# First batch's keys and queries placed pair by pair from SBUF to SBUF, first feed-forward loads a turn later, scores over 96 and 99 rows

## The chip, the cores and the metric

The kernel runs on one core of one Trainium2 chip. The metric is the device time of one execution in microseconds (us), as the median of the runs.

## The reference

For 16 batches of 256 tokens of width 256, the reference computes a cross-attention and a feed-forward net of eight experts:

```python
q = (layernorm(x) @ Wq + bq), k = concat([ctx1 @ Wk + bk, ctx2]), v = concat([ctx1 @ Wv + bv, ctx2])   # 16 heads of 16
x = x + softmax(q k^T / 4) v @ Wp + bp
y = layernorm(x)
cw = softmax(y @ w_router) * softmax(10 * y @ w_gating);  cw = cw / (sum(cw) + 1e-9)
out = x + sum over e of cw[e] * ((silu(y @ w_gate[e]) * (y @ w_up[e])) @ w_down[e])     # inner width 1024
```

Here x has 16 x 256 x 256 elements, ctx1 and ctx2 (fside_BxSxS_0 and ctx_1024) likewise, so a query sees 512 keys.

## The kernel before

Every matmul of 32-bit data is split into a high and a low part (names with _hi and _lo), and three products stand for one. The work is laid out in turns and steps. A turn b belongs to a batch of attention and has 32 steps; turns -2 and -1 prepare. Each engine runs its own program over the same turns and steps, in order, and they meet in semaphores, so an engine that waits holds back everything behind it in its program. A class Count holds a semaphore with the number of increments per batch, and turn.wait(engine, count, d, n) waits for the n-th of batch b + d.

In a step the attention does one score matmul eight items ahead (AHEAD = 8, line L803, queries by keys, into ps_s), whose row maximum VectorE takes (negmax, L1187), and one key matmul (L813, keys by queries, into ps_t), whose exponential ScalarE takes (L947). An item is a head and a half of the queries for the first, and a pair of heads and a quarter of the keys for the second; four items are a pair, and there are eight pairs (PAIRS). The maximum is not subtracted by an engine: POOL and TensorE turn it into three rows (mq, "qm"), which ScalarE writes below the queries in QTs, and KTs holds rows of ones in the same places, so that the key matmul subtracts it. Low parts of the exponentials (Pt_lo) and the products with the values follow.

KTs and QTs hold the operands in this form: in partitions 0 to 31, 32 to 63 and 64 to 95 the high, low and high part of the keys, and the high, high and low part of the queries, and from TOP = 96 on the three rows of the maximum with zeros below them. The score matmul contracts over 96 partitions, the key matmul over 128. The keys of a batch stand after their projection in kT_hi and kT_lo (two chunks of 128 partitions by 512 keys, each chunk with four pairs), the queries in qT_hi and qT_lo. SP stores both to memory (d_k, d_q: store_keys L439, store_queries L445) and loads them from there into KTs and QTs for four pairs at a time (place_keys L452 with 3 loads, place_queries L466 with 6). In turn -1 the two stores and the first placement are issued at steps 10 and 11, in the other turns at steps 14 to 19, and the second four pairs at steps 1 and 3 of the turn after.

Between these, a list written out by hand, ITEMS, says in which step a turn does its other parts, among them cT (step 1, ctx1 transposed for the next batch), k (step 4), v (9), xT (11), m (12, ctx2 transposed) and q (13). In turn -1 they come at the steps in FIRST_AT, cT, xT, k, m, q, v. They use two banks of PSUM in alternation (bank(one): ps_m or half of ps_o), and each waits until the item before it in the same bank has been read. ScalarE and VectorE take k out (L925, L1143) before their attention work of the same step, after they have waited for k_out, the store of the batch before.

In turn -2 SP issues the first loads: the four attention weights, biases, router weights, then three feed-forward weights (load_weights, the first unit, L531), then the constant rows of KTs from key_rows (32 rows, L432). POOL clears key_rows, QTs and others with memsets (L1199 to L1209) and VectorE writes the ones. The feed-forward net starts in turn 2 at step 19 and from there every step has one unit of it beside the attention; its first weights are taken out of stage_w by ScalarE at steps 4, 12 and 20 of turn 1. Before the scores of turn -1 TensorE runs 36 transposes that nobody reads (keep_busy).

Of the kernel before, what the change touches and what calls it, by code (L numbers as in the profile page):

```python
# [24 lines left out]
F32 = mybir.dt.float32  # L25
# [4 lines left out]
P = 128  # L30
# [6 lines left out]
def bass_xattn_moe_ffn_kernel(nc, x, ctx1, ctx2, Wq, bq, Wk, bk, Wv, bv, Wp, bp, w_router, w_gating,  # L37
# [15 lines left out]
    TOP = 3 * ROWS  # L53
    GP = PAIRS // 2
# [38 lines left out]
    with ExitStack() as ctx:  # L93
# [114 lines left out]
        rows_in = sem("rows_in"); rows_clear = sem("rows_clear")  # L208
# [15 lines left out]
        v_ps = Count("v_ps", 1); v_done = Count("v_done", 1)  # L224
        k_in = [Count(f"k_in{g}", 16 * 3) for g in range(2)]
# [21 lines left out]
        CONSTS = 7  # L247
        LAST = (START + FSTEPS) // STEPS

# [58 lines left out]
        for b in range(-2, LAST + 1):  # L308
            for step, name, k, d in items_of(b):
                joint = b * STEPS + step >= START  # L310
                one = joint or len(items) % 2 == 0
                items[b, step] = (name, k, d, one, last_in.get(one, []))
                last_in[one] = released(b, name, k, d)
                if not joint:
                    last_early = dict(last_in)
# [5 lines left out]
        def bank(one):  # L321

            return ps_m[:] if one else ps_o[:, 1, :]
# [83 lines left out]
        def _(eng):  # L407
            def first_loads():

                def load_bias(m):  # L410
                    if m < 2:
                        for c in range(DC):
                            eng.dma_start(bT[:, m, c:c + 1], (bq, bk)[m][bass.ds(c * P, P)].rearrange("(p o) -> p o", o=1)).then_inc(b_in[m], 16)
                    else:
                        eng.dma_start(bias[:, m - 2], (bv, bp)[m - 2].rearrange("(o n) -> o n", o=1)
                                      .broadcast_to([P, D])).then_inc(b_in[m], 16)

                for n, w in enumerate((Wk, Wv, Wq, Wp)):
                    if n == 2:
                        load_bias(1)  # L420
                        load_bias(2)
                    if n == 3:
                        eng.dma_start(VF[:, QT:KC, :], one(c2_v, Turn(-1), 1)).then_inc(c2_in.sem, 16)
                        load_bias(0)
                        load_bias(3)
                    eng.dma_start(wraw[:, n], w.rearrange("(c p) n -> p c n", p=P)).then_inc(w_in[n], 16)
                eng.dma_start(rraw[:, :, 0:E], w_router.rearrange("(c p) n -> p c n", p=P)).then_inc(w_in[4], 16)
                eng.dma_start(rraw[:, :, E:2 * E], w_gating.rearrange("(c p) n -> p c n", p=P)).then_inc(w_in[4], 16)
                for n in range(3):
                    load_weights(n, 0)  # L430
                eng.wait_ge(const_ready, CONSTS)
                eng.dma_start(KTs[TOP:P].bitcast(F32), key_rows[TOP:P].unsqueeze(1).broadcast_to([ROWS, PAIRS, NK])).then_inc(rows_in, 16)  # L432

# [12 lines left out]

            def place_keys(turn, d, g):

                turn.wait(eng, k_out, d, 32)
                turn.wait(eng, t_ps, d - 1, 2 * OCT * (g + 1))  # L450
                for slot, part in enumerate((0, 1, 0)):
                    eng.dma_start(KTs[slot * ROWS:(slot + 1) * ROWS, g * GP:(g + 1) * GP, :].bitcast(F32),  # L452
                                  d_k[turn.b + d, part, bass.ds(g * P, P)].rearrange("(a r) n -> r a n", r=ROWS)).then_inc(k_in[g].sem, 16)

            def place_queries(turn, d, g):

                turn.wait(eng, q_out, d, 32)
                turn.wait(eng, t_ps, d - 1, 2 * OCT * (g + 1))
                if turn.b == -1:
                    eng.wait_ge(const_ready, CONSTS)  # L460
# [10 lines left out]
            def body(turn):  # L471
                for step in range(STEPS):
# [28 lines left out]
                    first = turn.b == -1  # L501
                    if turn.has(1) and step == (10 if first else 14):
                        store_keys(turn, 1)
                    if turn.has(1) and step == (10 if first else 15):
                        store_queries(turn, 1)
                    if turn.has(1) and step == (11 if first else 17):
                        place_keys(turn, 1, 0)
                    if turn.has(1) and step == (11 if first else 19):
                        place_queries(turn, 1, 0)
                    if turn.has(0) and step == 1:  # L510
                        place_keys(turn, 0, 1)
                    if turn.has(0) and step == 3:
                        place_queries(turn, 0, 1)
# [62 lines left out]
        def _(pe):  # L576
# [177 lines left out]
            def body(turn):  # L754
                for step in range(STEPS):
# [37 lines left out]
                    if turn.has(d):  # L793
                        h, qt = i // QT, i % QT
                        if i % (4 * GP) == 0:
                            g = i // (4 * GP)
                            if turn.b + d == 0:
                                pe.wait_ge(rows_in, 16)
                            turn.wait(pe, k_in[g], d, k_in[g].per)
                            turn.wait(pe, q_in[g], d, q_in[g].per)  # L800
# [5 lines left out]
                    if turn.has(0):  # L806
                        i = step
                        pair, kc = i // KC, i % KC
                        if kc == 0:
                            turn.wait(pe, qm_done, 0, 2 * pair + 2)  # L810
                        j = turn.b * STEPS + i
                        wait_keys_read(pe, j)
                        pe.matmul(key_bank(j)[:], KTs[:, pair, kc * P:(kc + 1) * P],  # L813
                                  QTs[:, pair].rearrange("p h n -> p (h n)"),
                                  start=True, stop=True).then_inc(t_ps.sem, 1)
# [5 lines left out]
        def _(act):  # L821
# [45 lines left out]
            def body(turn):  # L867
                for step in range(STEPS):
# [49 lines left out]
                    if name in ("k", "q"):  # L918
# [4 lines left out]
                        turn.wait(act, used, 0, 32)  # L923
# [3 lines left out]
                    if name == "m":  # L927
                        turn.wait(act, m_ps, 1, 1)
                        turn.wait(act, k_out, 0, 32)
                        act.activation(kT_hi[:, :, N:NK], ps[:].rearrange("p (c n) -> p c n", n=N), ACT.Copy).then_inc(m_h.sem, 1)  # L930
                    if name == "qm":
                        turn.wait(act, qm_ps, d, k + 1)
                        for h in range(2):
                            act.activation(QTs[TOP:TOP + 3, k, h, :], ps[HS * h + ROWS:HS * h + ROWS + 3, 0:N],
# [18 lines left out]
        def _(dve):  # L953
# [113 lines left out]
            def body(turn):  # L1067
                for step in range(STEPS):
# [8 lines left out]
                    if turn.b == -2 and step == 0:  # L1077
                        dve.wait_ge(rows_clear, 1)
                        dve.memset(key_rows[TOP:TOP + 3, :], 1.0).then_inc(const_ready, 1)
# [55 lines left out]
                    if name in ("k", "q"):  # L1135
# [4 lines left out]
                        turn.wait(dve, used, 0, 32)  # L1140
# [5 lines left out]
                    if name == "m":  # L1146
                        turn.wait(dve, m_h, 1, 1)
                        turn.wait(dve, k_out, 0, 32)
# [49 lines left out]
        def _(pool):  # L1198
# [6 lines left out]
            pool.memset(key_rows[:], 0.0).then_inc(rows_clear, 1)  # L1205
# [127 lines left out]
```

## Time and profile before

| | |
|---|---|
| time, median of 3 runs | 2712.37 us (2711.29 to 2715.34) |
| the profiled execution, time and span | 2711.55 us, 2709.8 us |
| mean granted clock of TensorE | 0.991 |
| TensorE busy | 2660.4 us (98%) |
| VectorE busy | 2007.7 us (74%) |
| POOL busy | 1651.8 us (61%) |
| ScalarE busy | 1526.0 us (56%) |
| DMA engines' mean busy share by the main queue | 39.0% |
| chain that ended last | TensorE 94%, VectorE 4%, issue 1%, DMA 1% |

In a profile PE is TensorE's matmuls, PEld its weight loads, DVE VectorE, ACT ScalarE, SPq the queue of SP that issues transfers. L803 is a line of the kernel. The busy time is summed over the span; the chain is followed back from the last instruction through what released each step. A clock of 1.00 is 2.4 GHz and 0.50 is 1.2 GHz.

### The profile page before, as it was taken

The page shows a single profiled execution, that of the slowest core. Times are in us where ns is not written, and L with a number is a line of the kernel's source. Part 1 is how long each engine was busy: PE and PEld are TensorE (multiplying, and loading weights), DVE is VectorE, ACT ScalarE, POOL GpSimd, SP SyncE. Part 2 cuts the span into 40 slices and gives each one's busy share as a digit, 9 for nine tenths or more (in the row PEclk, how much of TensorE's full clock was granted, in tenths as well). Part 3 has the DMA queues.
Part 4 walks back from the last instruction along what each step waited for, and adds up shares of the span by engine and source line. Part 5 has one row for each costly group of instructions (what it writes and reads, how often), then busy time and mean ns, then how long its engine had stood idle before and what let it go on. Part 6 is the DMA issues. An engine that isn't in the chain of part 4 may idle for free.

```text
span 2709.8 us, 46807 instructions
## 1 busy us (share of the span) xinstructions
PE 2660.4 (98%) x15969; PEld 2184.3 (81%) x15969; DVE 2007.7 (74%) x3303; ACT 1526.0 (56%) x2887; POOL 1651.8 (61%) x1837
## 2 busy tenths in 40 slices
PE   6899999999999999999999999999999999999998
PEld 5578888888888888888888888888888888888887
DVE  6987777777778777777777777777787777655554
ACT  4655555555555555555555555555555555544443
POOL 4766666666656666566666566666566666655554
PEclk8899999999999999999999999999999999999999
DMA  6344434444333443433434433444333442333332
GB/s 166 101 112 122 127 100 118 132 120 123 115 118 115 120 126 115 127 109 112 131 115 131 120 116 108 125 122 131 113 105 114 126 122 88 97 107 113 108 102 82
DMA packets 298427, 315.44 MB, mean 116 GB/s; under 512 B 22096, under 2 KB 269264, under 8 KB 298192
## 3 DMA queue, kind: packets, MB, share of 16 engines
q1 hardware_dynamic: 298192, 312.45, 39.0%
q8 instruction: 130, 2.13, 0.3%
q14 instruction: 105, 0.86, 0.1%
HBM read 278.15 MB, written 33.69 MB: 115 GB/s over the span
## 4 chain that ended last, share of the span: by engine, by line
PE 94%; DVE 4%; issue 1%; DMA 1%; POOL 0%; ACT 0%; SPq 0%; POOLq 0%; DVEq 0%; ACTq 0%
PE ps_s L706 26%; PE ps_t L706 26%; PE ps_o L740 25%; PE ps_s L803 4%; PE ps_t L813 4%; PE ps_a L782 2%; PE ps_a L784 2%; PE ps_m L586 1%; PE ps_m L615 1%; DVE negmax L1187 1%; PE ps_m L604 1%; DVE Pt_lo L1059 1%; PE ps_m L659 0%; DMA d_k<-kT_lo 0%; PE ps_m L677 0%
## 5 line engine op out<-in xcount | busy, mean ns | idle before, releaser
L969 DVE SCALAR_TENSOR_TENSOR hf<-hf,ps_s 128x512 f32<-128x512 f32 x512 | 350.2, 684 | 326.7 <-ACT hf L827 324.8
L833 ACT ACTIVATE h_hi<-ps_t 128x512 fp32r<-128x512 f32 x512 | 306.1, 598 | 440.2 <-DVE ps_t L976 440.2
L1221 POOL TENSOR_TENSOR wg_lo<-stage_w,wg_hi 128x512 fp32r<-128x512 f32 x256 | 330.9, 1292 | 339.5 <-ACT wg_hi L840 337.9
L827 ACT ACTIVATE hf<-ps_s 128x512 f32<-128x512 f32 x512 | 306.4, 598 | 410.5 <-PE ps_s L706 410.5
L981 DVE TENSOR_TENSOR h_lo<-ps_t,h_hi 128x512 fp32r<-128x512 f32 x512 | 353.0, 689 | 211.9 <-ACT h_hi L833 205.6
L740 PE MATMUL ps_o<-h_lo,wd_hi 128*128 128x512 f32 x1024 | 400.1, 391 | 0.0
L740 PE MATMUL ps_o<-h_hi,wd_hi 128*128 128x512 f32 x1024 | 398.5, 389 | 0.9 <-DVE h_lo L981 0.9
L740 PE MATMUL ps_o<-h_hi,wd_lo 128*128 128x512 f32 x1024 | 398.4, 389 | 0.0
L976 DVE TENSOR_TENSOR ps_t<-hf,ps_t 128x512 f32<-128x512 f32 x512 | 356.4, 696 | 52.9 <-PE ps_t L706 6.2
L1221 POOL TENSOR_TENSOR wd_lo<-stage_w,wd_hi 128x512 fp32r<-128x512 f32 x256 | 330.8, 1292 | 93.0 <-ACT wd_hi L840 93.0
L947 ACT ACTIVATE Pt<-ps_t 128x512 f32<-128x512 f32 x512 | 305.8, 598 | 142.1 <-PE ps_t L813 134.1
L1187 DVE TENSOR_REDUCE negmax<-ps_s 128x1 f32<-128x512 f32 x512 | 347.5, 681 | 23.4 <-PE ps_s L803 22.6
L1286 POOL TENSOR_TENSOR Pt_lo<-Pt 128x512 f16<-128x512 f32 x256 | 278.8, 1089 | 130.2 <-ACT Pt L947 126.8
L1221 POOL TENSOR_TENSOR wu_lo<-stage_w,wu_hi 128x512 fp32r<-128x512 f32 x256 | 333.6, 1303 | 0.0
L706 PE MATMUL ps_s<-xh,wg_hi 128*128 128x512 f32 x1024 | 320.5, 394 | 0.9 <-DVE negmax L1187 0.9
L706 PE MATMUL ps_s<-xh,wg_lo 128*128 128x512 f32 x1024 | 319.1, 392 | 0.0
L706 PE MATMUL ps_t<-xh,wu_hi 128*128 128x512 f32 x1024 | 317.5, 391 | 1.2 <-DVE h_lo L981 1.2
L706 PE MATMUL ps_s<-xl,wg_hi 128*128 128x512 f32 x1024 | 317.7, 391 | 0.0
L706 PE MATMUL ps_t<-xh,wu_lo 128*128 128x512 f32 x1024 | 316.2, 390 | 0.0
L706 PE MATMUL ps_t<-xl,wu_hi 128*128 128x512 f32 x1024 | 315.3, 389 | 0.0
L803 PE MATMUL ps_s<-KTs,QTs 96*128 96x512 f32 x512 | 231.7, 453 | 26.6 <-DVE negmax L1187 14.2
L1059 DVE TENSOR_TENSOR Pt_lo<-Pt 128x512 f16<-128x512 f32 x256 | 251.7, 983 | 1.6 <-ACT Pt L947 1.6
(208 smaller groups left out, 4734.3 us busy)
## 6 DMA issues: line engine op xcount, KB each, us to landing
stage_w<-in_L_ffn_w_gate_dram SPq DMA_DIRECT2D x256, 256.0 KB, 2.8
stage_w<-in_L_ffn_w_up_dram SPq DMA_DIRECT2D x256, 256.0 KB, 3.1
stage_w<-in_L_ffn_w_down_dram SPq DMA_DIRECT2D x256, 256.0 KB, 2.8
KTs<-d_k SPq DMA_DIRECT2D x96, 256.0 KB, 4.9
cwb<-d_cw SPq DMA_DIRECT2D x64, 256.0 KB, 3.6
QTs<-d_q SPq DMA_DIRECT2D x192, 64.0 KB, 2.7
X<-in_x_dram SPq DMA_DIRECT2D x32, 256.0 KB, 4.5
d_k<-kT_hi SPq DMA_DIRECT2D x16, 512.0 KB, 4.1
```

The source lines that it names most:

```text
L706: mm = pe.matmul(ps[:], wt[:, c, q * P:(q + 1) * P], tok[:, c].rearrange("p k n -> p (k n)"), start=(n == 0), stop=(n == 3 * DC - 1))
L740: mm = pe.matmul(ps_o[:, c, :], wt[:, q, c * P:(c + 1) * P], hid[:], start=(at == 0 and n == 0), stop=(at == EXPERT - 1 and n == 2))
L803: pe.matmul(score_bank(j)[:], QTs[0:TOP, h // 2, h % 2, qt * P:(qt + 1) * P], KTs[0:TOP, h // 2, :], start=True, stop=True).then_inc(s_ps. ...
L827: act.activation(hf[:], ps_g[:], ACT.Tanh, scale=0.5).then_inc(tanh_done, 1)
L833: act.activation(h_hi[f % FC][:], ps_u[:], ACT.Copy).then_inc(hh_done, 1)
L947: act.activation(Pt[i % RING][:], key_bank(turn.b * STEPS + i)[:], ACT.Exp).then_inc(exp_done.sem, 1)
L969: dve.scalar_tensor_tensor(out=hf[:], in0=hf[:], scalar=1.0, in1=ps_g[:], op0=ALU.add, op1=ALU.mult).then_inc(gate_done, 1)
L976: dve.tensor_tensor(ps_u[:], hf[:], ps_u[:], ALU.mult).then_inc(hf_done, 1)
L981: dve.tensor_tensor(h_lo[f % FC][:], ps_u[:], h_hi[f % FC][:].bitcast(F32), ALU.subtract).then_inc(hl_done, 1)
L1187: dve.tensor_reduce(negmax[:, (i // 4) % 2, i % 4:i % 4 + 1], score_bank((turn.b + d) * STEPS + i)[:], AX.X, ALU.max, negate=True).then_in ...
L1221: pool.tensor_tensor(lo[:], raw_weights(n), hi[:].bitcast(F32), ALU.subtract).then_inc(wl_done, 1)
L1286: pool.tensor_tensor(Pt_lo[slot][:], Pt[slot][:], Pt[slot][:].bitcast(BF16)[:, 1::2], ALU.subtract).then_inc(lo_pool.sem, 1)
```

## The change

For batch 0, the way of keys and queries through memory is replaced. A new function, place_first, issues at step 10 of turn -1 for each of the eight pairs three copies of keys and six of queries from kT and qT to KTs and QTs, SBUF to SBUF, 72 in all; a copy of keys has 32 partitions by 512 elements and one of queries 16 by 256. TensorE waits for each pair on a semaphore of its own (first_in). In turn 0 ScalarE and VectorE wait for all eight before they overwrite the source for batch 1 (wait_stored). For the other batches the stores and loads are as before; their counts begin one batch later, hence d - 1. The item q of turn -1 gets the bank ps_t[1] and waits for no other. The three first feed-forward loads move from turn -2 to steps 20, 21 and 22 of turn 0. The constant rows are 3 instead of 32, loaded without a wait for POOL's memsets and waited for at the first key matmul, POOL doesn't clear key_rows, and the key matmul contracts over 99 partitions (USED) instead of 128; the score matmul has 96 as before.

```diff
+    USED = TOP + 3
...
+        def wait_stored(eng, turn, count):
+
+            if turn.b == 0:
+                for arrived in first_in:
+                    eng.wait_ge(arrived, 16 * 9)
+            else:
+                turn.wait(eng, count, -1, 32)
...
+                if (b, name) == (-1, "q"):
+                    items[b, step] = (name, k, d, None, [])
+                    continue
...
-            return ps_m[:] if one else ps_o[:, 1, :]
+            return ps_t[1][:] if one is None else ps_m[:] if one else ps_o[:, 1, :]
...
-                for n in range(3):
-                    load_weights(n, 0)
-                eng.wait_ge(const_ready, CONSTS)
-                eng.dma_start(KTs[TOP:P].bitcast(F32), key_rows[TOP:P].unsqueeze(1).broadcast_to([ROWS, PAIRS, NK])).then_inc(rows_in, 16)
+                eng.wait_ge(rows_set, 1)
+                eng.dma_start(KTs[TOP:USED].bitcast(F32), key_rows[TOP:USED].unsqueeze(1).broadcast_to([3, PAIRS, NK])).then_inc(rows_in, 16)
...
+            def place_first():
+
+                eng.wait_ge(k_l.sem, 2)
+                eng.wait_ge(m_l.sem, 1)
+                for pair in range(PAIRS):
+                    m, at = pair // GP, pair % GP * ROWS
+                    for slot, part in enumerate((kT_hi, kT_lo, kT_hi)):
+                        eng.dma_start(KTs[slot * ROWS:(slot + 1) * ROWS, pair, :].bitcast(F32),
+                                      part[at:at + ROWS, m, :].bitcast(F32)).then_inc(first_in[pair], 16)
+                    if pair == 0:
+                        eng.wait_ge(q_l.sem, 2)
+                        eng.wait_ge(const_ready, CONSTS)
+                    for slot, part in enumerate((qT_hi, qT_hi, qT_lo)):
+                        for h in range(2):
+                            to, row = slot * ROWS + h * HD, at + h * HD
+                            eng.dma_start(QTs[to:to + HD, pair, h, :].bitcast(F32),
+                                          part[row:row + HD, m, :].bitcast(F32)).then_inc(first_in[pair], 16)
...
-                turn.wait(eng, k_out, d, 32)
+                turn.wait(eng, k_out, d - 1, 32)
...
+                    if turn.b == -1 and step == 10:
+                        place_first()
+                    if turn.b == 0 and step >= 20 and step - 20 < 3:
+                        load_weights(step - 20, 0)
+                    if turn.b >= 0 and turn.has(1):
+                        if step == 14:
+                            store_keys(turn, 1)
...
-                        if i % (4 * GP) == 0:
+                        if turn.b + d == 0:
+                            if i % 4 == 0:
+                                pe.wait_ge(first_in[i // 4], 16 * 9)
+                        elif i % (4 * GP) == 0:
...
+                        if turn.b == 0 and i == 0:
+                            pe.wait_ge(rows_in, 16)
...
-                        pe.matmul(key_bank(j)[:], KTs[:, pair, kc * P:(kc + 1) * P],
-                                  QTs[:, pair].rearrange("p h n -> p (h n)"),
+                        pe.matmul(key_bank(j)[:], KTs[0:USED, pair, kc * P:(kc + 1) * P],
+                                  QTs[0:USED, pair].rearrange("p h n -> p (h n)"),
...
-                        turn.wait(act, used, 0, 32)
+                        wait_stored(act, turn, used)
...
-                        dve.wait_ge(rows_clear, 1)
-                        dve.memset(key_rows[TOP:TOP + 3, :], 1.0).then_inc(const_ready, 1)
+                        dve.memset(key_rows[TOP:USED, :], 1.0).then_inc(rows_set, 1)
...
-                        turn.wait(dve, used, 0, 32)
+                        wait_stored(dve, turn, used)
...
-            pool.memset(key_rows[:], 0.0).then_inc(rows_clear, 1)
```

## Rows read from the trace of the kernel before

**Rows 1.** The page, its first line.

```profile
span 2709.8 us, 46807 instructions
```

**Rows 2.** Windows: stretch, length, busy of PE PEld DVE ACT POOL, clock, DMA, GB/s.

```profile
0.00:200.00 200.00, 158.76 (x1339) 116.63 (x1340) 161.42 (x317) 112.18 (x235) 121.80 (x202) 0.90 0.48 127
200.00:2500.00 2300.00, 2299.63 (x13747) 1901.91 (x13746) 1734.73 (x2825) 1319.69 (x2487) 1423.22 (x1552) 1.00 0.39 117
```

**Rows 3.** Chain of waits, 12 to 60 us: start, length, what.

```profile
13.16 0.61 DVE kT_lo L1149
...
14.26 9.93 DMA d_k<-kT_lo
...
27.88 3.64 DMA QTs<-d_q
...
31.65 0.78 PE ps_s L803
...
39.88 0.43 PE ps_t L813
...
45.70 0.84 ACT kT_hi L925 x2
...
47.52 1.20 DVE negmax L1187 x2
...
52.42 0.23 PE ps_t L813
```

**Rows 4.** Timeline up to 17 us: start, length, instruction, [idle before, releaser].

```profile
1.54 0.53 POOL L1205 MEMSET key_rows<- 128x512 f32 x1
...
4.61 1.72 DVE L1018 TENSOR_SCALAR mv<-mv 128x2 f32<-128x2 f32 x1
...
5.54 0.77 POOL L1209 MEMSET mq<- 128x256 bf16 x2
...
13.21 0.50 PE L615 MATMUL ps_m<-xT_hi,wq_hi 128*128 128x256 f32 x2 [1.56 <-DVE kT_lo L1143]
...
15.93 0.88 DVE L1143 SCALAR_TENSOR_TENSOR qT_lo<-ps_m,bT,qT_hi 128x256 fp32r<-128x256 f32 x2 [2.18 <-ACT qT_hi L925]
```

**Rows 5.** Timeline of SP's queue: start, time to issue, transfer, count.

```profile
2.76 0.94 SPq L413 DMA_DIRECT2D bT<-in_L_xattn_bk_dram  x2
...
9.19 0.47 SPq L531 DMA_DIRECT2D stage_w<-in_L_ffn_w_down_dram  x1
...
13.85 0.37 SPq L439 DMA_DIRECT2D d_k<-kT_hi  x1
...
25.58 2.72 SPq L466 DMA_DIRECT2D QTs<-d_q  x6
...
38.29 2.81 SPq L466 DMA_DIRECT2D QTs<-d_q  x6
...
64.65 3.72 SPq L466 DMA_DIRECT2D QTs<-d_q  x6
...
122.72 0.32 SPq L495 DMA_DIRECT2D d_cw<-cwT  x1
```

**Rows 6.** The tile QTs up to 140 us, last line.

```profile
DMA to landing us min/median/max: 2.2/3.7/5.0
```

**Rows 7.** Windows of 2 us, 40 to 50 us, as rows 2.

```profile
40.00:42.00 2.00, 2.00 (x9) 1.38 (x8) 0.78 (x3) 1.45 (x3) 1.75 (x5) 0.50 0.61 181
42.00:44.00 2.00, 2.00 (x7) 1.23 (x5) 2.00 (x4) 1.88 (x5) 0.68 (x2) 0.52 0.50 144
44.00:46.00 2.00, 2.00 (x16) 1.86 (x16) 1.73 (x3) 1.18 (x4) 1.85 (x2) 1.00 0.00 0
...
48.00:50.00 2.00, 1.33 (x4) 0.60 (x4) 2.00 (x5) 1.64 (x5) 1.14 (x3) 1.00 0.00 0
```

**Rows 8.** Weight loads of lines L803 and L813: ns min/median/max.

```profile
L803 PEld LDWEIGHTS ps_s<-KTs,QTs x512: 186/188/338, 31.6 to 2319.7; 96*128 96x128 f32 x171
...
L813 PEld LDWEIGHTS ps_t<-QTs,KTs x512: 186/191/338, 39.2 to 2356.4; 128*128 128x128 f32 x171
```

More of the change, by code:

```diff
@@ L207, in bass_xattn_moe_ffn_kernel @@
         w_in = [sem(f"w_in{n}") for n in range(5)]; b_in = [sem(f"b_in{m}") for m in range(4)]; b_scaled = sem("b_scaled")
-        rows_in = sem("rows_in"); rows_clear = sem("rows_clear")
+        rows_in = sem("rows_in"); rows_set = sem("rows_set")
         ident_done = sem("ident_done"); const_ready = sem("const_ready")
@@ L224, in bass_xattn_moe_ffn_kernel @@
         v_ps = Count("v_ps", 1); v_done = Count("v_done", 1)
+        first_in = [sem(f"first_in{p}") for p in range(PAIRS)]
         k_in = [Count(f"k_in{g}", 16 * 3) for g in range(2)]
@@ L245, in bass_xattn_moe_ffn_kernel @@
         cwT_ps = Count("cwT_ps", 1); cwT_done = Count("cwT_done", 1)
-        CONSTS = 7
+        CONSTS = 6
         LAST = (START + FSTEPS) // STEPS
+        def wait_stored(eng, turn, count):
[4 more added lines that the diff above has]
+                turn.wait(eng, count, -1, 32)
         class Turn:
@@ L455, in place_queries @@
             def place_queries(turn, d, g):
-                turn.wait(eng, q_out, d, 32)
+                turn.wait(eng, q_out, d - 1, 32)
                 turn.wait(eng, t_ps, d - 1, 2 * OCT * (g + 1))
-                if turn.b == -1:
-                    eng.wait_ge(const_ready, CONSTS)
                 pairs = slice(g * GP, (g + 1) * GP)
@@ L500, in body @@
                         combine_ahead(f)
[L501 to L513, printed above, removed]
+                    if turn.b == -1 and step == 10:
[5 more added lines that the diff above has]
+                            store_keys(turn, 1)
+                        if step == 15:
+                            store_queries(turn, 1)
+                        if step == 17:
+                            place_keys(turn, 1, 0)
+                        if step == 19:
+                            place_queries(turn, 1, 0)
+                    if turn.b >= 1 and turn.has(0):
+                        if step == 1:
+                            place_keys(turn, 0, 1)
+                        if step == 3:
+                            place_queries(turn, 0, 1)
                     if step in (10, 12) and turn.closed is not None:
@@ L794, in body @@
                         h, qt = i // QT, i % QT
-                        if i % (4 * GP) == 0:
+                        if turn.b + d == 0:
+                            if i % 4 == 0:
+                                pe.wait_ge(first_in[i // 4], 16 * 9)
+                        elif i % (4 * GP) == 0:
                             g = i // (4 * GP)
[L797 to L800, printed above, removed]
+                            turn.wait(pe, k_in[g], d - 1, k_in[g].per)
+                            turn.wait(pe, q_in[g], d - 1, q_in[g].per)
                         j = (turn.b + d) * STEPS + i
@@ L928, in body @@
                         turn.wait(act, m_ps, 1, 1)
-                        turn.wait(act, k_out, 0, 32)
+                        wait_stored(act, turn, k_out)
                         act.activation(kT_hi[:, :, N:NK], ps[:].rearrange("p (c n) -> p c n", n=N), ACT.Copy).then_inc(m_h.sem, 1)
@@ L933, in body @@
                         for h in range(2):
-                            act.activation(QTs[TOP:TOP + 3, k, h, :], ps[HS * h + ROWS:HS * h + ROWS + 3, 0:N],
+                            act.activation(QTs[TOP:USED, k, h, :], ps[HS * h + ROWS:HS * h + ROWS + 3, 0:N],
                                            ACT.Copy).then_inc(qm_done.sem, 1)
@@ L1147, in body @@
                         turn.wait(dve, m_h, 1, 1)
-                        turn.wait(dve, k_out, 0, 32)
+                        wait_stored(dve, turn, k_out)
                         dve.tensor_tensor(kT_lo[:, :, N:NK], ps[:].rearrange("p (c n) -> p c n", n=N),
```

## The prediction

> **What bounds the kernel now.** I read the page first: the span is 2709.8 us [rows 1], and the profiled execution took 2711.55 us, 1.75 us of it around the span. That is 0.82 us under the median of the three runs, 2712.37 us, so I add 0.8 us at the end. Next the windows: from 200 us to 2500 us TensorE is busy for 2299.63 of 2300 us, so nothing there waits, and an edit that moves only loads can gain nothing there. In the first 200 us TensorE is busy 158.76 us [rows 2]. So what this change gives or takes is a shift of the first turns, carried unchanged to the end.
>
> Then the chain of waits over the start [rows 3]. The low half of the first keys is ready at 13.77 us (0.61 us from 13.16). The chain then goes through the store of the keys (9.93 us), through the issues of the placement, through a load of queries (3.64 us), and the first score starts at 31.65 us. Turn 0 begins about 39.88 us; ScalarE takes the keys of batch 1 out of their bank at 45.70 us. That last row is my yardstick: whatever shifts it shifts the end, for VectorE's low half of the same keys and its next maximum stand behind it, and TensorE's next scores behind those; VectorE's maximum comes 0.98 us after the 0.84 us of kT_hi, at 47.52 us.
>
> **The change, part by part.**
>
> *Earlier keys.* A small VectorE operation on mv, two elements wide, takes 1.72 us from 4.61; it ends at 6.33 us, when POOL's last memset ends (5.54 + 0.77 = 6.31). So I read it as held up by POOL, and taking out the memset of key_rows (0.53 us) shortens that row of memsets by about 0.5 us [rows 4]. Everything up to the keys follows those operations, so I put SP's start on them at 13.85 - 0.5 = 13.35 us [rows 5]. At worst that gain is 0.
>
> *Earlier queries.* The first query matmul waited 1.56 us for kT_lo, because both used one bank [rows 4]. With a bank of its own it starts 1.56 + 0.5 us earlier, and qT_lo ends at 16.81 - 2.06 = 14.75 us [rows 4].
>
> *The placement.* Six large store and load steps through memory become 8 pairs x 9 = 72 DMAs on SP, in one row, with SP doing nothing else meanwhile. What does one cost to issue? Six loads of queries take 2.72 us at 25.58 and 2.81 us at 38.29; with one more gap of 0.04 us (from 13.85 + 0.37 to 14.26 [rows 3, 5]) that is 0.460 and 0.475 each, in the mean 0.467 us. Two bias columns of 0.5 KB take 0.94 us, also 0.47 each, so size hardly matters. Lowest row: 0.32 us for d_cw, whose tile spans 8 partitions, with the gap 0.36. Highest row: 3.72 us for six behind a backlog, 0.62. I take 0.467, for these have 16 or 32 partitions like the query loads (16) and are seldom behind a backlog. The three keys of pair 0 end at 13.35 + 1.4 = 14.75, just when the queries are ready, so SP doesn't wait. The last of the 72 starts at 13.35 + 71 x 0.467 = 46.51 us.
>
> Its landing: query loads of 64 KB land in 2.2 us at least, 3.7 in the median, 5.0 at most, in the first 140 us [rows 6]. SBUF to SBUF doesn't occur. The last one has 16 KB and little beside it (288 KB per 4.2 us is 69 GB/s), so I take 2.3, with 2.2 and 5.0 as ends. All is placed at 48.81 us.
>
> The Trainium skill (DMA: Bandwidth & Descriptors, section Anatomy of one DMA, given for the other DMA path) puts a fixed cost of about 2.0 us on a DMA besides its bytes; as an estimate that would make the shift below 0.3 us smaller, and no row here shows it for this path.
>
> *Who waits.* The first scores profit. Pair 0 is issued by 17.6 us and lands at 13.35 + 8 x 0.467 + 2.3 = 19.4 us, and pair 1 4.2 us later, at 23.6; four more scores with the normalisation between take about 4.9 us, so turn 0 begins near 28.5 us, 11.4 us earlier than at 39.88. Each further pair comes every 4.2 us, and turn 0 takes one only every four steps (5.8 us from 39.88 to 45.70), so the scores don't wait. But the keys of batch 1 at step 4 of turn 0 overwrite kT_hi and kT_lo, which are now the source of the placement, and wait_stored makes ScalarE and VectorE wait there for all 72. They arrive at 28.5 + 5.8 = 34.3 us and wait until 48.8. Behind that wait stand ScalarE's exponential of step 4 and VectorE's maximum of score 12, and TensorE stops two scores later, since it needs both. So the gain of 11.4 us is given back whole, and more: kT_hi starts at 48.86 us in place of 45.70, 3.2 us later. The break-even is an issue of 0.467 - 3.16 / 71 = 0.42 us.
>
> *The clock of TensorE.* In the kernel before it is granted 0.50 (1.2 GHz) in the stretch 40 to 42 us and 0.52 in the next, and 1.00 (2.4 GHz) from 44 us on [rows 7]. TensorE had stood idle until 31.65 us, worked with gaps until about 40, and without a gap from there to the rise. At the low level a key matmul takes 0.43 us of the chain, at the high one 0.23 [rows 3]. The slow steps before 45.70 no longer cost anything, as they lie ahead of the wait. Instead TensorE stands still for over 10 us and starts at low clock right after it, where before it ran at 1.00. If the clock again rises after about 3.9 us of gapless work (40.1 to 44), that is 1.95 us of full-speed work lost, less the 0.67 us in which TensorE was idle in the stretch 48 to 50 us [rows 7]: 1.3 us. Bounds: 0 if VectorE hides it, 3.5 us if the rise takes twice as long.
>
> *What is behind the 72 on SP.* The loads of x and ctx1 for batch 2 now start at about 47 us; x is wanted at step 23 of turn 0, 19 steps of 1.45 us (5.8 / 4) after the wait at step 4, and ctx1 in turn 1. The load of ctx2 waits for POOL's split at step 7 anyway. Cost 0. If that cover were gone, one landing of about 3 us.
>
> *The feed-forward loads* leave the start (three issues, the last at 9.19 us [rows 5], 768 KB) and come at steps 20 to 22 of turn 0, three issues of 0.47 us, ahead of the load of X1, which is then 1.4 us later, and wanted four steps on. ScalarE wants the first weights at step 4 of turn 1, sixteen steps after. Cost 0; the start they leave is priced by the short landings above. The constant rows shrink from 512 KB to 48 KB and are issued ahead of the inputs: 0.
>
> *Contraction over 99 rows instead of 128.* Weight loads of 96 and of 128 rows take 188 and 191 ns in the median [rows 8]. The stage from 200 us on would move only if the matmul did, and it streams the same 512 columns. I take 0; with 512 of them even the 3 ns would be 1.5 us, the lower bound.
>
> **Sum.** 3.2 + 1.3 = 4.5 us on 2711.55 gives 2716.0, and with the 0.8 us to the median 2716.8 us, 0.17% slower. What a measurement of this kernel can tell from no change is about 0.2%, 5.4 us, so the likeliest outcome is not to be told apart, on the slow side.
>
> **Rivals.**
>
> *Issues are cheap: faster.* If a DMA of 16 or 32 partitions is issued in 0.36 us, like d_cw, everything is placed at 13.35 + 25.6 + 2.3 = 41.2 us, kT_hi starts 4.5 us earlier than before, and with the 1.3 us for the clock and 1.5 us from the weight loads the time is 2712.4 - 4.5 + 1.3 - 1.5 = 2707.7 us. It is faster than before below 0.42 us (below 0.40 if the clock costs 1.3). For it: the row of d_cw. Against: all rows with 16 or more partitions, even the 0.5 KB ones. The Trainium skill says that the sequencer's time to start a DMA is usually small beside the DMA itself (DMA: Bandwidth & Descriptors, section Issuing engines are not separate DMA queues); the trace does not agree for such sizes, 0.47 us each against a landing of 2.2. Chance of a gain over 0.2%: 0.08.
>
> *The wait doesn't bite.* If step 4 came after the last landing anyway, the 11.4 us would stay, 2701.0 us. It would need turn 0 to begin 14 us later than I find. This is part of the 0.08.
>
> *The queue backs up or the clock stays low.* With 0.51 us per issue, as the issue of 0.47 us at 9.19 gives with its gap [rows 5], the shift is 3.2 + 3.1 = 6.3 us; with up to 3.5 us for the clock it is 9.8 us: 2722.2 us. At 0.62 us it would be 14 us and more, 2727. For it: six loads that took 3.72 us [rows 5]. Against: that was behind 1.5 MB of stores, just issued. Chance of over 5.4 us in all: 0.36.
>
> *The same within 0.2%:* 0.56, which holds the forecast and small gains at issues of 0.40 to 0.42. Taken together I expect 2710 to 2722.
>
> **What would show it.** In the profile after: 72 DMAs on SP from about 13.4 to 47 us with 0.467 us spacing; the first score at about 19.5 us; a wait of ScalarE and VectorE of about 14 us ahead of the kT_hi of batch 1, which starts at 48.9 us; TensorE's clock at half when it resumes; the same durations for the matmuls on KTs and QTs; TensorE still without a gap from 200 us on. I am wrong if the spacing of issues is below 0.42 or above 0.52, if small copies queue and land later than 3 us, or if the low clock lasts longer than 4 us after the wait.

## The result and the profile after

The changed kernel takes 2732.05 us (median of 6 runs) against 2711.14 us for the kernel before (6 runs): 20.9 us slower, ratio 1.0075 with a 95% interval of 1.0062 to 1.0088. The prediction had 2716.8 us, 2710 to 2722 us, and most of its chance on no difference that can be told. The sign and the mechanism are right, the size is four to five times the forecast, and the time lies outside the range.

The page after, its first lines and its clock row, answers to [rows 1]:

```profile
span 2732.3 us, 46878 instructions
## 1 busy us (share of the span) xinstructions
PE 2669.1 (98%) x15969; PEld 2194.4 (80%) x15969; DVE 2006.9 (73%) x3303; ACT 1526.7 (56%) x2887; POOL 1653.3 (61%) x1836
...
PEclk7889999999999999999999999999999999999999
```

The busy times are those of before within 9 us of TensorE; the span is 22.5 us longer. So the work is the same and something waits. The stage from 250 us on shows where it isn't (columns as in [rows 2]):

```profile
40.00:50.00 10.00, 1.99 (x39) 1.45 (x38) 0.00 (x0) 0.00 (x0) 0.73 (x4) 0.81 0.17 43
50.00:60.00 10.00, 0.00 (x0) 0.00 (x0) 0.00 (x0) 0.00 (x0) 0.00 (x0) 0.50 0.22 54
60.00:64.00 4.00, 0.00 (x0) 0.00 (x0) 0.94 (x3) 2.32 (x6) 0.94 (x1) 0.50 0.47 141
64.00:70.00 6.00, 5.42 (x18) 4.53 (x19) 4.34 (x7) 2.59 (x6) 4.05 (x9) 0.50 0.04 11
70.00:74.00 4.00, 3.98 (x52) 2.96 (x50) 3.51 (x7) 2.91 (x7) 1.40 (x2) 0.99 0.17 53
...
250.00:2500.00 2250.00, 2249.62 (x13497) 1861.80 (x13496) 1700.35 (x2771) 1293.01 (x2438) 1398.36 (x1526) 1.00 0.40 118
```

From 50 to 60 us every engine is idle, with the DMA engines busy 0.22 of their time. TensorE comes back at a clock of 0.50 and stays there up to 70 us. What everybody waits for stands in the timelines of SP's queue (start, time to issue), of ScalarE and of TensorE, which answer to [rows 5] and [rows 3]:

```profile
13.39 0.62 SPq L465 DMA_DIRECT2D KTs<-kT_hi  x1
14.06 0.59 SPq L465 DMA_DIRECT2D KTs<-kT_lo  x1
14.69 1.65 SPq L465 DMA_DIRECT2D KTs<-kT_hi  x1
16.43 2.43 SPq L473 DMA_DIRECT2D QTs<-qT_hi  x4
18.91 1.22 SPq L473 DMA_DIRECT2D QTs<-qT_lo  x2
20.17 0.59 SPq L465 DMA_DIRECT2D KTs<-kT_hi  x1
...
59.07 1.22 SPq L473 DMA_DIRECT2D QTs<-qT_lo  x2
60.34 0.58 SPq L506 DMA_DIRECT2D X<-in_x_dram  x1
...
21.39 0.73 PE L836 MATMUL ps_s<-KTs,QTs 96*128 96x512 f32 x2 [2.43 <-DMA QTs<-qT_lo]
...
61.65 0.84 ACT L960 ACTIVATE kT_hi<-ps_o,bT 128x256 fp32r<-128x256 f32 x2 [22.93 <-DMA QTs<-qT_lo]
```

The copies begin at 13.39 us, as forecast (13.35), and each takes 0.59 us to issue and 0.04 of gap, 0.63 us, where I had 0.467. Pair 1 starts at 20.17 and takes 5.7 us, like every pair but two (pair 0 is held up by 1.1 us, pair 6 by 0.4 us, from causes that the trace doesn't show). The last of the 72 starts at 59.70 us and lands 1.84 us later. ScalarE had waited 22.93 us for it, and kT_hi of batch 1 starts at 61.65 us: 15.95 us later than the 45.70 of [rows 3]. The first score did start 10.26 us earlier, at 21.39; TensorE then waited 2.79 us for the copies of pair 1 and 2.10 us for those of pair 2, and the first key matmul started at 33.38 us, 6.3 us earlier than before.

The rest, 22.5 - 15.95 = 6.6 us, is lost between 61.65 us and the first unit of the feed-forward net, which starts at 191.69 us against 169.17. From here on I call "low time" the sum over windows of 2 us of 2 x 2 x (1 - clock), the time at 1.2 GHz. Between 40 and 240 us it is 24.4 us in the kernel before and 64.8 us after, of which 18 lie in the stall, where they cost nothing; the other 47 are nearly twice those of before.

### The profile page after: what moved, and what is told of

Its sections match the earlier page's. It is cut to its first block, busy times and chain, and to the rows that moved or that the text cites. A ratio compares the mean times of both kernels' runs of the same rounds, so it can differ in the third digit from the quotient of the medians.

```text
span 2732.3 us, 46878 instructions
## 1 busy us (share of the span) xinstructions
PE 2669.1 (98%) x15969; PEld 2194.4 (80%) x15969; DVE 2006.9 (73%) x3303; ACT 1526.7 (56%) x2887; POOL 1653.3 (61%) x1836
## 4 chain that ended last, share of the span: by engine, by line
PE 93%; DVE 3%; SPq 2%; issue 1%; POOL 1%; ACT 0%; DMA 0%; POOLq 0%; DVEq 0%; ACTq 0%
PE ps_s L738 26%; PE ps_t L738 25%; PE ps_o L772 25%; PE ps_s L836 4%; PE ps_t L848 4%; PE ps_a L814 2%; PE ps_a L816 2%; PE ps_m L618 1%; PE ps_m L647 1%; PE ps_m L636 1%; SPq L473 1%; DVE negmax L1221 1%; SPq L465 1%; PE ps_m L691 0%; DVE Pt_lo L1094 0%
```

## The experiments

**The copies alone.** The theory is that the 72 copies are the whole loss; the rival, that the late loads or the 99 rows carry a part. In outline, against the changed kernel:

```diff
 # batch 0 again: store_keys, store_queries, place_keys, place_queries as in the kernel before
-def place_first():
...
+store_keys(turn, 1); store_queries(turn, 1); place_keys(turn, 1, 0); place_queries(turn, 1, 0)
```

> Batch 0 goes through memory as before; all other parts of the change are kept (late feed-forward loads, own bank for q, short constant rows, 99 rows). If the 72 copies are the whole loss, the stores start at 13.4 us as in the changed kernel, land in about 4 us instead of 9.9 because the weight loads are gone, and the first score starts at about 25.5 us against 31.65: about 6 us faster than before, 2705 us. If late loads or the 99 rows carry a part of the loss, it is slower than that by that part, at or above 2711 us.

It took 2711.76 us (11 runs), ratio 0.9996, 0.9987 to 1.0005: the same as before. So the whole loss belongs to the copies: with them the same kernel takes 20.3 us more. But the gain of 6 us isn't there either. The first score starts at 27.69 us, 4.0 us earlier, and kT_hi of batch 1 at 43.02, 2.7 us earlier, yet the feed-forward net starts at 169.53 us, 0.4 us later. The low time between 40 and 240 us is 44.8 us.

**What an issue costs.** Eight groups of six DMAs at the end of the kernel before, with nothing beside them.

```diff
+            priced(0, mem(128, NK), kt(128, NK))    # SBUF to memory
+            priced(1, to(32, NK), mem(32, NK))      # memory to SBUF
+            priced(2, to(32, NK), kt(32, NK))       # SBUF to SBUF
+            priced(3, to(16, N), mem(16, N))        # memory to SBUF
+            priced(4, to(16, N), kt(16, N))         # SBUF to SBUF, and 5 (128, NK), 6 (8, NK)
+            priced(7, to(128, NK), mem(128, NK))    # memory to SBUF
```

> The kernel before with eight groups of six DMAs each issued by SP alone at its very end: memory to SBUF and SBUF to SBUF, each with 16 partitions by 256, 32 by 512 and 128 by 512, SBUF to SBUF with 8 by 512, and SBUF to memory with 128 by 512. The time of the kernel itself says nothing. Theory A (both ends in SBUF cost the issue 0.59 us): all SBUF to SBUF groups at 0.59 us each whatever their size, all memory to SBUF ones at 0.43 to 0.47. Theory B (few partitions cost it): the 16 and 32 partition groups at 0.59 from either source, the 128 ones at 0.43 to 0.47. Theory C (the queue was behind): all at 0.43 to 0.47 here.

The timeline of SP's queue of this kernel, in the order of the groups (the fifth row is the groups 4, 5 and 6 with the waits between them):

```profile
2714.49 3.08 SPq L579 DMA_DIRECT2D scr_d<-kT_hi  x6
2719.96 2.64 SPq L579 DMA_DIRECT2D KTs<-scr_d  x6
2724.03 3.74 SPq L579 DMA_DIRECT2D KTs<-kT_hi  x6
2729.18 2.62 SPq L579 DMA_DIRECT2D KTs<-scr_d  x6
2733.07 14.86 SPq L579 DMA_DIRECT2D KTs<-kT_hi  x18
2749.27 2.92 SPq L579 DMA_DIRECT2D KTs<-scr_d  x6
```

With 32 partitions, six loads from memory take 2.64 us and six copies from SBUF to SBUF 3.74 us: 0.44 and 0.62 us each. Loads of 16 partitions cost the same 0.44 (2.62 / 6), those of 128 partitions 0.49, stores 0.51. Theory A holds: it is the pair of SBUF addresses, not the few partitions. The groups of the fifth row are told apart by asking for the tile KTs in a window for each: 16 x 256, 128 x 512 and 8 x 512, with the least, median and greatest ns of an issue:

```profile
L579 SPq DMA_DIRECT2D KTs<-kT_hi x6: 513/589/591, 2733.1 to 2736.2; - x6
L579 SPq DMA_DIRECT2D KTs<-kT_hi x6: 527/609/613, 2738.0 to 2741.2; - x6
L579 SPq DMA_DIRECT2D KTs<-kT_hi x6: 624/630/736, 2743.8 to 2747.3; - x6
```

From 16 to 256 KB a copy takes 0.59 to 0.61 us to issue, and with 8 partitions no less but 0.63. The same view gives 590 ns for the group of 32 x 512, and 420 to 424 ns for the three groups of loads.

**Two issuers.** Is it the issuer, or the DMA engines behind it?

```diff
-                        place_first()
+                        place_first(range(GP))             # SP: pairs 0 to 3
...
+                        for pair in range(GP, PAIRS):      # ScalarE, step 10 of turn -1: pairs 4 to 7
+                            ... act.dma_start(KTs[...], part[at:at + ROWS, m, :]) ...
```

> The changed kernel with the 36 copies of pairs 4 to 7 issued by ScalarE while SP issues the other 36. Issue theory: each row of 36 takes 23 us (0.63 each), both are over at about 37 us, the scores run on and ScalarE starts turn 0 near 38 us, kT_hi of batch 1 starts at 44 to 46 us, and the time is 2711 to 2717 us. If the 16 DMA engines or SBUF's own port take the 0.6 us per copy, two issuers gain nothing: kT_hi stays at about 61 us and the time at 2732 us.

It took 2721.14 us, ratio 1.0034 (1.0022 to 1.0047): between the two kernels. Two rows of its timeline, of ScalarE's queue and of SP's at the same time:

```profile
22.59 2.54 ACTq L949 DMA_DIRECT2D QTs<-qT_hi  x4
...
21.61 2.53 SPq L473 DMA_DIRECT2D QTs<-qT_hi  x4
```

Both issue at 0.64 us each side by side (5.78 us for a pair of heads), and all 72 are out by 38 us: the price is paid at each issuer and its queue, and the DMA engines carry twice the rate. My figures, 44 to 46 us for kT_hi and 2711 to 2717 us for the time, were missed: kT_hi starts at 51.74 us. ScalarE's own work (splits of values and weights, the rows of the maximum) now stood behind its 36 issues, and turn 0 began only after it; TensorE, idle meanwhile, was granted a clock of 0.50 from 40 to 50 us.

**The wait.** Batch 0 in tiles of its own, so that batch 1 overwrites nothing.

```diff
+        k0 = [t[:].rearrange("p c k n -> p c (k n)") for t in (xh[1], xl[1])]
+        q0 = [t[:].rearrange("p (c n) -> p c n", n=N) for t in h_hi]
...
-            if turn.b == 0:
-                for arrived in first_in:
-                    eng.wait_ge(arrived, 16 * 9)
```

> The changed kernel, but batch 0 has its keys and queries in tiles that the feed-forward net uses later, so that nobody waits in turn 0 before kT_hi of batch 1. If that wait is what gives the gain back, kT_hi of batch 1 starts at about 35 to 38 us. SP is still issuing until 60 us, so the load of ctx2 for the item m at step 12 comes at about 61.4 us and is the next thing waited for: kT_hi of m at 65 us against 55.86 before, about 9 us slower than before plus the clock, 2720 to 2725 us. If the wait has no part, 2732 us. If nothing else on SP matters, 2702 us.

It took 2723.93 us, ratio 1.0046 (1.0033 to 1.006). kT_hi of batch 1 starts at 40.37 us, 21 us earlier than in the changed kernel, though later than the expected 35 to 38. Then the next customer of SP is late, as forecast; the timelines of SP, TensorE and ScalarE:

```profile
62.22 0.47 SPq L516 DMA_DIRECT2D VF<-in_ctx_dram  x1
...
65.83 0.44 PE L636 MATMUL ps_m<-ident,VF 128*128 128x128 f32 x1 [16.05 <-DMA VF<-in_ctx_dram]
...
66.95 0.60 ACT L970 ACTIVATE kT_hi<-ps_m 128x512 fp32r<-128x512 f32 x1 [16.17 <-PE ps_m L636]
```

So the stall has two causes in a row, the wait for the source and the load of ctx2 behind the copies. The next kernel takes away both.

```diff
-                        place_first()
+                        place_first((0, 1, 2, 3))
+                    if turn.b == 0 and step in (4, 6, 9, 13):
+                        place_first(({4: 4, 6: 5, 9: 6, 13: 7}[step],))
```

> The changed kernel with batch 0 in its own tiles, as in e4_own_tiles, and the copies of pairs 4 to 7 issued at steps 4, 6, 9 and 13 of turn 0, between the loads that SP owes to others, ctx2 among them. If the wait and the row of issues are the whole trouble, kT_hi of batch 1 starts at about 40.4 us as in e4_own_tiles (before: 45.70), the load of ctx2 starts at about 47 to 50 us and nothing waits for it long, and the time is 2 to 6 us under before, 2706 to 2710 us, less whatever the clock takes. If SP is simply overloaded by 45 us of issues, xT_hi and q of batch 1 are again late and the time stays above 2715 us.

It took 2718.48 us against 2713.03 in the same session, ratio 1.0015 (1.0006 to 1.0024): still not faster. q of batch 1 starts at 57.62 us, 0.4 us ahead of the kernel before (58.06), so the stall is gone. But the copies run on until 62.8 us, the last load of queries of batch 1 comes after them, TensorE waits 4.81 us for it (0.79 us at the same place before), and cT of batch 2 is at 89.95 us against 83.97. The low time is 51.9 us. SP is overloaded, and the time is above 2715 us, as in the second of the expected outcomes; but xT_hi and q of batch 1 are not late, the placement of batch 1 is.

**The clock.** First TensorE was kept busy in the stall alone.

```diff
+                    if (turn.b, step) == (0, 6):
+                        for p in range(3, 7):
+                            pe.wait_ge(first_in[p], 16 * 9)
+                            for _ in range(44):
+                                pe.transpose(ps_a[:, 0:P], ident[:], ident[:])
```

> The changed kernel, with 44 unread transposes of TensorE after the arrival of each of the pairs 3 to 6 in the stall of turn 0. kT_hi of batch 1 stays at about 61.6 us. If the low clock after the stall costs what I think, the clock is 1.00 at 61 to 70 us, and the 2.1 us lost between kT_hi and xT_hi of batch 1 come back, with up to 4 us of the later part: 2726 to 2730 us. If the clock has no part in it, the time stays at 2732 us.

It took 2733.98 us, ratio 1.0081 (1.0068 to 1.0094). This tells nothing: the transposes ended before the wait did, and the clock was 1.00 up to 64 us and then 0.55, just when the work came back. The second try holds it:

> As e3_kept_busy, but with 44 to 48 unread transposes per pair and 25 more after the last pair, so that TensorE has no gap left before the real work comes back. Clock theory: the clock stays 1.00 over the resumption, and the distance from kT_hi to xT_hi of batch 1 falls from 11.3 us to the 9.2 us of the kernel before, 2 us of the loss; the later part of turns 0 and 1 may still fall low. If the distance stays at 11 us, something other than the clock slows these steps.

Windows of this kernel (columns as in [rows 2]):

```profile
60.00:64.00 4.00, 3.37 (x32) 3.14 (x30) 0.00 (x0) 1.02 (x3) 0.00 (x0) 1.00 0.32 86
64.00:70.00 6.00, 5.41 (x38) 4.33 (x35) 5.22 (x10) 3.84 (x9) 4.25 (x7) 1.00 0.12 43
```

The clock is now 1.00, and from kT_hi to xT_hi of batch 1 it is 72.63 - 62.98 = 9.65 us, where the changed kernel has 72.94 - 61.65 = 11.29 and the kernel before 54.91 - 45.70 = 9.21. So the low clock costs 1.6 us right after the stall; the 0.4 us left to the kernel before are not the clock's. The time is 2732.05 us all the same (ratio 1.0066, 1.0054 to 1.0079, in a session where the kernel before took 2713.03). The trace shows two reasons. kT_hi itself starts 1.3 us later than in the changed kernel, as the row of issues was held up for longer, so at xT_hi only 0.3 us is left; and the clock falls again later, with 34 us of low time between 80 and 160 us (31 in the changed kernel). So this kernel shows what the low clock costs on the spot, not what it costs at the end. The next two hold the clock over turns 0 to 2 up to the feed-forward net:

```diff
+                    if turn.has(0) and turn.b * STEPS + step < START - 1:
+                        j = turn.b * STEPS + step
+                        wait_keys_read(pe, j)
+                        for _ in range(3):
+                            pe.transpose(key_bank(j)[:, 0:P], ident[:], ident[:])
```

> The kernel before with three unread transposes of TensorE in each step of turns 0 to 2 up to the feed-forward net, ahead of the score matmul, in the time in which TensorE waits for VectorE. It has about 24 us of half clock lost in stretches between 40 and 240 us. If these cost real time there, holding the clock up gives back 2 to 5 us: 2706 to 2710 us. If TensorE is not what those turns wait for, the time stays at 2711 to 2712 us or rises by the transposes, up to 0.1 us a step, 8 us.

> e1_via_memory (everything of the change but the 72 copies) with the same three transposes per step. There the first score came 4.0 us earlier than before, and this was lost again by the start of the feed-forward net, with 45 us of low-clock share between 40 and 240 us against 24 before. Clock theory: the gain survives, 2703 to 2707 us, and it beats e7_before_filled by about 3 us. Otherwise both have the same time.

The kernel before with three unread transposes per step took 2710.59 us (11 runs), ratio 0.9989 (0.998 to 0.9998): a gain within what is hard to tell. e1_via_memory with them took 2707.09 us (9 runs), ratio 0.9976 (0.9966 to 0.9985), 4.7 us less than without. The clock held: low time 0.3 and 0.0 us. Two stretches of e1_via_memory and the same of its filled form:

```profile
108.00:116.00 8.00, 7.27 (x53) 5.24 (x51) 7.31 (x17) 4.73 (x12) 3.91 (x8) 0.55 0.99 270
116.00:124.00 8.00, 7.65 (x55) 4.45 (x56) 7.97 (x21) 4.13 (x10) 7.08 (x13) 0.50 0.27 72
```

```profile
108.00:116.00 8.00, 7.16 (x91) 5.44 (x91) 7.93 (x20) 5.71 (x13) 5.19 (x12) 1.00 0.99 245
116.00:124.00 8.00, 6.68 (x82) 4.94 (x79) 7.97 (x19) 4.61 (x11) 7.35 (x11) 1.00 0.22 70
```

Of the 91 and 82 matmuls 15 and 18 are unread transposes, so TensorE does 76 and 64 of its own instead of 53 and 55. From 108 to 116 us this feeds VectorE, which is busy for 7.93 us instead of 7.31; from 116 to 124 us VectorE is full in both kernels. Over longer stretches, from the start of kT_hi of batch 1 to that of batch 2, and from there to the feed-forward net (us; e8_after_filled follows below):

| kernel | kT_hi 1 to kT_hi 2 | kT_hi 2 to the net | low time, 40 to 240 us |
|---|---|---|---|
| before | 42.56 | 80.91 | 24.4 |
| e1_via_memory | 42.93 | 83.58 | 44.8 |
| after | 45.93 | 84.11 | 64.8 (18 in the stall) |
| e7_before_filled | 45.21 | 78.84 | 0.3 |
| e6_via_memory_filled | 44.86 | 78.71 | 0.0 |
| e8_after_filled | 46.67 | 78.23 | 3.4 |

So the transposes are not free: between the two kT_hi e7_before_filled and e6_via_memory_filled take 2 to 3 us longer than without them, and behind that the held clock gives 2 to 5 us back. Where the clock is held, the second stretch is the same within 0.7 us, whatever came before it. With the clock held, the head start of 2.6 us at kT_hi (41.36 against 43.97) is still 3.1 us at the feed-forward net (164.93 against 168.02). This is where the gain of e1_via_memory had gone: it was lost to a clock that stayed low longer. Its 11 executions say the same: 2707.5 and 2708.2 us at a mean clock of 0.990, 2712.6 to 2714.0 us at 0.986 and 0.987.

Now the changed kernel itself with both kinds of filling:

> The changed kernel with TensorE kept busy all along: the transposes of e3b_kept_busy_longer in the stall and the three per step of e7_before_filled. With the clock at 1.00 on both sides, what is left of the loss is the row of issues alone: kT_hi of batch 1 at about 62 us against 43.97 in e7_before_filled, 18 us, so 2710.6 + 18 = 2728.5 us. A time of 2732 us or more would mean that the low clock cost nothing; one under 2724 us, that a part of the 18 us is made up elsewhere.

It took 2728.48 us, ratio 1.006 (1.0048 to 1.0073). kT_hi of batch 1 starts at 62.12 us, 18.15 us after that of e7_before_filled, the feed-forward net 19.0 us after, and the time is 17.9 us longer (2728.48 - 2710.59). With the clock held on both sides, but for 3.4 us of low time at 102 to 106 us here, the row of issues explains the loss, and the shift is carried through to within 1 us.

The loss without filling, 20.9 us, is 3 us larger. But in the sum of times this part doesn't come with the copies. By the copies and the transposes of the stall alone e8_after_filled differs from e6_via_memory_filled, and is 21.4 us slower (2728.48 - 2707.09); without filling the copies cost 20.3 us (2732.05 - 2711.76). That is nearly the same. What differs is the rest of the change, worth 3.5 us with the clock held and nothing that can be told without. These kernels ran in four sessions, between which the kernel before moved by up to 1.9 us, so a difference of 1 us between them says nothing.

**What made the store of the first keys slow.** Before, the keys took 9.9 us to land in memory; in e1_via_memory 5.5.

```diff
+                for n in range(3):
+                    load_weights(n, 0)
                 eng.wait_ge(rows_set, 1)
-                    if turn.b == 0 and step >= 20 and step - 20 < 3:
-                        load_weights(step - 20, 0)
```

> e6_via_memory_filled with the three first feed-forward loads back at the start. If their 768 KB are what made the store of the keys take 9.9 us before, it takes that again, the first score falls back to about 31 us, and the time is that of e7_before_filled, 2710.6 us. If the shorter constant rows (48 KB for 512) did it, the gain stays, 2707 us.

It took 2707.86 us (11 runs), ratio 0.9984 (0.9975 to 0.9993), 0.8 us more than e6_via_memory_filled, whose interval it overlaps. The store lands in 5.89 us, with the loads postponed in 5.05 (e6_via_memory_filled) and 5.51 us (e1_via_memory), and in 8.11 us in e7_before_filled, whose code up to there is that of the kernel before with its 9.93. So the postponed loads give at most 0.8 us, which is less than the 1.8 us between those two executions of the same code, and 2 us and more came with the constant rows, 48 KB in place of 512. That their size did it is the likeliest reading; POOL's memset and the bank of q changed with them and were not tested apart.

**A version that beats both.** Only the pair that is wanted first goes from SBUF to SBUF.

```diff
+                    if first and step == 10:        # between the stores: 3 copies of keys, 6 of queries, pair 0
+                        for slot, part in enumerate((kT_hi, kT_lo, kT_hi)):
+                            eng.dma_start(KTs[slot * ROWS:(slot + 1) * ROWS, 0, :].bitcast(F32),
+                                          part[0:ROWS, 0, :].bitcast(F32)).then_inc(first_in, 16)
```

> e6_via_memory_filled with only pair 0 of batch 0 copied from SBUF to SBUF (9 copies, 5.7 us), between the stores and the loads; pairs 1 to 3 and 4 to 7 come through memory. The first four scores start at about 23.5 us instead of 27.1, pair 1 comes at about 28.5, so turn 0 begins 1 to 3 us earlier: 2704 to 2706 us. If the nine issues only delay the loads behind them on SP, the second pair is late and the time stays at 2707 us or rises by 1 to 2 us.

It took 2704.19 us (7 runs, 2703.45 to 2705.75), ratio 0.9972 (0.9961 to 0.9982), and is the fastest here. Its first scores and those of pair 1, in TensorE's timeline:

```profile
23.84 1.22 PE L828 MATMUL ps_s<-KTs,QTs 96*128 96x512 f32 x2 [4.88 <-DMA QTs<-qT_lo]
...
28.68 1.19 PE L828 MATMUL ps_s<-KTs,QTs 96*128 96x512 f32 x2 [1.66 <-DMA QTs<-d_q]
```

Nine copies (5.7 us of SP) stand between the stores and the loads. A part of that is hidden behind the landing of the stores: the loads start 3.7 us later than in e6_via_memory_filled (22.62 us for 18.88), and TensorE waits 1.66 us for them. But the first score starts at 23.84 us instead of 26.34, and kT_hi of batch 1 at 39.03 us instead of 41.36. All seven times are below the lowest of e6_via_memory_filled (2706.25 us), which ran in another session.

## Why the prediction was wrong, step by step

**What bounds it, and the yardstick:** right. Most of the loss is seen at kT_hi of batch 1 (15.95 us of 22.5), and the stage behind is gapless in both kernels.

**Start of the copies:** right, 13.39 us for 13.35. The small operation on mv shrank from 1.72 to 1.27 us with POOL's memset gone. The queries were ready a little before SP had a use for them.

**The price of an issue:** this step failed. It was the term "I take 0.467, for these have 16 or 32 partitions like the query loads". It measured 0.633 us, 71 of them with two short hold-ups 46.3 us instead of 33.2. My range of issues from rows, 0.36 to 0.62 us, nearly held it, but I kept the upper end for a backed-up queue and chose by the number of partitions, when what was new about these DMAs was their source. The text itself says that SBUF to SBUF doesn't occur before, and I let that widen the landing alone. The landing was 1.84 us for 2.3. Together 12.8 us more than forecast at kT_hi (15.95 for 3.2). It is the term of the sum that was mis-sized; the sum itself, with 0.633 us put in, gives 15 us.

**Who waits:** right, with its places: the wait of ScalarE and VectorE before kT_hi (22.9 us instead of 14.5). That "the scores don't wait" was wrong at this price: TensorE waited 2.10 us for the copies of pair 2, and turn 0 began at 33.38 us in place of the forecast 28.5. This cost nothing, as it lies ahead of the wait for all 72. That the load of ctx2 costs nothing was right for this kernel, but it is the next wait as soon as the first is taken away, 16.05 us in e4_own_tiles.

**The clock:** the mechanism was right and the size too small. Forecast 1.3 us, for a clock that stays at half for 3.9 us of work; it stayed there for 5.4 us (64.58 to 70), which is one of the signs of being wrong that the prediction names, and cost 1.6 to 2.1 us right after the stall. Up to the feed-forward net the clock fell more often than before, and with the stall's part 6.6 us were lost there in the profiled execution. Not all of this is due to the copies: e1_via_memory, without the stall, loses 3.0 us over the same ground. That the shift is "carried unchanged to the end" was the wrong part of the first step: e1_via_memory lost its whole head start on the way.

**The late loads and the constant rows, at 0:** no kernel here shows them to be wrong for the changed kernel, which has no store of the first keys for them to speed up. In the kernels that go through memory, all of the change but the copies is worth 3.5 us with the clock held (2707.09 against 2710.59), most of it by the quicker store; that such a gain was to be had without the copies the prediction didn't see.

**99 rows:** 0, as forecast. The matmuls on L848 take 389/395 ns (minimum, median) with 99 rows, as L813 did with 128.

**The chances:** 0.36 for slower by more than 0.2% was the case that came, for the price, not for the backed-up queue that carried it. The slow rival's end, 0.62 us per issue, was given with "14 us and more" and 2727 us, and lay outside the range of 2710 to 2722 us that was to hold what I expect: the range left out its own rival's end.

## What to carry to other kernels

A path through memory with few large DMAs can be faster than many small copies that stay on the chip: the issuer is a serial resource, so count issues times their price, and take the price from a row with the same kind of source and destination. A wait for "all copied" turns the end of such a row into a barrier, and whatever the same queue owes to others is late next. Where TensorE is not the bound but not far from it (from 40 to 170 us before, VectorE is busy for 93% and TensorE for 82%), a small head start can be lost to a lower clock of TensorE. Compare versions with the clock held too, and count what the filling itself costs.

## What the runs showed of the hardware

A DMA with both ends in SBUF took 0.59 us to issue on SP (0.61 with 128 partitions, 0.63 with 8), and 0.60 on SP and 0.61 on ScalarE's queue with both issuing at once. Six in a row took 3.74 us, 0.62 each, against 0.44 to 0.49 each from memory to SBUF and 0.51 from SBUF to memory. The copies landed in 1.8 us (16 KB) to 2.5 us (256 KB), counted from the start of their issue.

In turns 0 to 2, up to the feed-forward net, the granted clock of TensorE fell to half again and again, for 3 to 17 us at a time: 24.4 us of low time in the kernel before, 44.8 in e1_via_memory, which does almost the same work. From kT_hi of batch 1 to the net TensorE was busy for 81% of the time in the kernel before. Ahead of the longest fall, from 108 to 125 us in e1_via_memory, it was busy for 1.81 of 4 us; ahead of the falls at 112 and 122 us in the kernel before, for 3.29 and 2.46 of 4 us. Three transposes of 128 columns per step, with which it was busy for 91%, removed nearly all of it (0.0 and 0.3 us in e6_via_memory_filled and e7_before_filled, 3.4 in e8_after_filled). What decides in which stretch it falls was not found; between executions of the changed kernel, all with a mean clock of 0.984, the time varied by 6 us.
